# Four narrow products of a fused attention and FFN kernel on Trainium2: from 256 moving columns to the columns that are used

## The chip, the cores and the metric

The kernel runs on one core of one Trainium2 chip. The time is device time in microseconds of one launch: 1570.47 us, the median of three runs (1569.87 to 1570.59).

## What is computed

The reference takes x (16 x 64 tokens of 512 features) and a context of the same size through eight residual layers; every layer first normalises x. Cut to what the change touches:

```python
x = x + L0_xattn(layernorm(x), ctx, ...)      # 32 heads, 4 kv heads
x = x + L0_ffn(layernorm(x), ...)             # base + 28 LoRA experts of rank 8, top 2
x = x + L1_xattn(layernorm(x), ctx, ...)
x = x + L1_ffn(layernorm(x), ...)             # base + 8 LoRA experts of rank 8, top 2
x = x + L2_xattn(layernorm(x), ctx, ctx)      # linear attention over the context
x = x + L2_ffn(layernorm(x), ...)             # 4 LoRA experts of rank 16, top 2
x = x + L3_xattn(layernorm(x), ctx, ...)      # one head of 512, keys of the own batch
x = x + L3_ffn(layernorm(x), ...)             # dense where similarity to 64 centroids is high

# L2 attention, the context product
kvs = einsum('bnhd,bnhe->bhde', softmax(k, over n), v)
# L2 FFN, the gate: 4 router logits and the 4*16 hidden values of the experts
logits = flat @ router_w.T;  mid = einsum('tf,erf->ter', flat, A)
# L3 attention, the scores
scores = einsum('btf,bsf->bts', Q, K) * scale
# L3 FFN, the similarity
dots = softmax(x @ centroids.T / TEMPERATURE)
```

## The kernel before

The 1024 tokens are eight tiles (NT = 8) of 128, two batches of 64 in each. x stays on the chip in `x_res` from the first layer to the last. A product of two fp32 numbers is made in three passes: each operand is split into a high and a low part, and `PASSES` names high x high, high x low and low x high. The contraction over 512 features is four slices (KT = 4), so a product of one tile is a group of 4 x 3 = 12 matmuls, each with its own weight load of 128 columns. ScalarE writes the high part of an operand, VectorE or GpSimd the low part (the helper line L1721 on VectorE, L1275 on ScalarE, L488 on GpSimd), and a semaphore counts tiles that are ready.

Each engine has its own instruction list, written out in the order in which it runs. On TensorE the order around the change is this.

- Both large attention layers (L0, L1) end at about 1300 us; the change does not touch them. The second FFN follows, with a gate of 72 columns (`gate_product`, L720), a dense product of 512 columns (L733) and an expert product (L971).
- `middle_step(t)` then interleaves three stages. For tile t it transposes exp(context) (L1044) and multiplies it with the context (L1080, `psK2`); for tile t-2 it multiplies the queries with the result (L1071 to L1073, 12 matmuls of 144 and 128 columns) and transposes the outcome (L1095). For tile e = t-5 it runs the gate of the third FFN (L720, out to `psSO`), and for e-1 the transposed hidden values (L955) and the expert product (L971, three matmuls of 512). For tile n = t-9 it runs the key product of the last attention (L1008, 512 columns). Transposes of normalised x are L706.
- `cross_attention` runs the last two layers over tiles p: `scores` (L1113), `q_transpose` (L1124), `q_proj` (L1137, 512 columns), a bias matmul (L1102), `k_transpose` (L1016), `p_transpose` (L1145), `similarity` (L1164), `attend` (L1152) and `dense` (L1181, 512 columns).

Four products in these stages move 256 columns for each matmul, though fewer are read:

- The context product L1080 needs its own tile's 128 columns; `two_tiles(t)` gives it two tiles of 128, and VectorE reads half of `psK2` (L2124).
- The gate of the third FFN needs 4 + 64 = 68 columns; `f.moving` is 2 * P for it, and the width for the other two.
- The scores L1113 need the 128 keys of their own tile; `kT3_pair` gives those of two tiles, and `own_scores` picks the half. For that the product waits until the keys of the next tile are there too.
- The similarity L1164 needs 64 centroids; the slice is 4 * S wide.

Of the kernel before, what the change touches and what calls it, by code (L numbers as in the profile page):

```python
# [5 lines left out]
P = 128  # L6
B, S, D = 16, 64, 512
TOK = B * S
NT = TOK // P
# [74 lines left out]
def build(nc, io):  # L84
# [94 lines left out]
    class Ffn:  # L179


        def __init__(self, index, ln, E, R, dense, scale, wkv_n, wo_n):
            self.index, self.ln, self.E, self.R = index, ln, E, R
            self.done = index * NT
            self.dense, self.scale = dense, scale
            self.width = E + E * R
            self.moving = self.width if dense else 2 * P
            self.parts = 2 if E * R > P else 1
            self.rows = E * R // self.parts
            self.wkv_n, self.wo_n = wkv_n, wo_n  # L190
# [40 lines left out]
    def lat(hl, k, n):  # L231
        return hT[:, hl, k, n, 1:3].rearrange("p b t -> p (b t)")
# [12 lines left out]
    def kT3(hl, n):  # L245
        return hT[:, hl, :, n, 0:4:3, :]

    def kT3_pair(hl, n, k):
        first = min(n, NT - 2)
        return hT[:, hl, k, first:first + 2, 0:4:3, :]  # L250

    def own_scores(n, b):
        at = (n == NT - 1) * P + b * S
        return psO[b * S:(b + 1) * S, 0, at:at + S]

    def two_by_two(t):
        return t[:].rearrange("p (b j c) -> p b j c", b=2, j=2)
# [47 lines left out]
    def gate_bank(f, n):  # L305
        return psS if f.index == 2 else psQ
# [7 lines left out]
    kvs_r = v1[:].rearrange("p a h c -> p (a h c)")[:, 0:4 * (P + GRP)].rearrange("p (a h c) -> p a h c", a=2, h=2)  # L314
    out_T = psTP[:].rearrange("p a (c t) -> p (a c) t", c=2)
    r_sum, y_T = k_sb[:, 0:S], prob[:]
    psE, psK2, psKT = psSO[:, 1], psSO[:, 2, 0:2 * P], psSO[:, 2]
    hidT = oT

    k3, k_in = prob, stage_q[:, 3]  # L320
# [373 lines left out]
    def _(pe):  # L694
# [14 lines left out]
        def gate_product(f, t):  # L709

            s, done = FS, f.done
            pe.wait_ge(LNS[f.ln]["lo"], ln_at(f.ln, t + 1))
            need(pe, s["hid"], done + t)
            if f.index == 2 and t == 0:
                pe.wait_ge(s["x_add"], done)
            if t == 0:
                pe.wait_ge(ld["wkv_lo"], f.wkv_n)
            for k in range(KT):
                for i, (xl, wl) in enumerate(PASSES):
                    m = mm(gate_bank(f, t)[:, 0:f.moving], lat(xl, k, t),  # L720
                           wkv[:, wl, k // 2, k % 2 * f.width:k % 2 * f.width + f.moving],
                           start=k == 0 and i == 0, stop=k == KT - 1 and i == 2)
            m.then_inc(s["gate_a"], 1)

# [272 lines left out]
            if 0 <= u < NT:  # L997
                experts(f, u)

        def two_tiles(n):  # L1000
            first = min(n, NT - 2)
            return slice(first * P, (first + 2) * P)

        def k_product(n):
            need(pe, N3["k_in"], n)
            for k in range(KT):
# [26 lines left out]
        def middle_step(t):  # L1033

            s, f, e, n = M, FF[2], t - 5, t - 9
            if 0 <= e - 1 < NT:
                if e == 5:
                    pe.wait_ge(s["y"], NT)
                hidden_transpose(f, e - 1)
            if t < NT:  # L1040
                pe.wait_ge(s["e"], t + 1)
                need(pe, s["eT_lo"], t)
                for k in range(KT):
                    i = tr(psE[:, k * P:(k + 1) * P], stage_q[:, t % 4, k * P:(k + 1) * P], ident[:])  # L1044
                i.then_inc(s["e_tr"], 1)
            if 0 <= t - 4 < NT:
                def free():
                    if t == 4:
                        pe.wait_ge(FS["hid"], 2 * NT)
                    need(pe, LNS[5]["lo"], ln_at(5, t - 4))  # L1050
                ln_transpose(5, t - 4, free)
            if 0 <= e < NT:
                if e <= 4:
                    need(pe, FS["hidT_lo"], f.done + e)
                gate_product(f, e)
            if 0 <= e - 1 < NT:
                experts(f, e - 1)
            if 0 <= n - 1 < NT:
                if n == 1:
                    pe.wait_ge(LNS[6]["lo"], ln_at(6, 2))  # L1060
                k_transpose(n - 1)
            if 0 <= t - 2 < NT:
                u = t - 2
                pe.wait_ge(s["q_lo"], u + 1)
                pe.wait_ge(s["kvs_lo"], u + 1)
                need(pe, s["y"], u)
                if u == 0:
                    pe.wait_ge(FS["hidT_lo"], 2 * NT)
                for c in range(KT):
                    q_of = lambda hl: q_e[:, hl, c * P:(c + 1) * P]  # L1070
                    mm(out_T[:, c, 0:P + GRP], q_of(HI), kvs_r[:, u % 2, HI, :], start=True, stop=False)  # L1071
                    mm(out_T[:, c, 0:P], q_of(HI), kvs_r[:, u % 2, LO, 0:P], start=False, stop=False)
                    m = mm(out_T[:, c, 0:P + GRP], q_of(LO), kvs_r[:, u % 2, HI, :], start=False, stop=True)  # L1073
                m.then_inc(s["out"], 1)
            if t < NT:
                pe.wait_ge(s["eT_lo"], t + 1)
                need(pe, s["kvs"], t)
                for k in range(KT):
                    for i, (el, cl) in enumerate(PASSES):
                        m = mm(psK2, eT[:, el, k, :], ctxT[:, cl, k, two_tiles(t)],  # L1080
                               start=k == 0 and i == 0, stop=k == KT - 1 and i == 2)
                m.then_inc(s["kv"], 1)
            if 0 <= n < NT:
                if n == 0:
                    pe.wait_ge(LNS[6]["lo"], ln_at(6, 1))
                    pe.wait_ge(ld["wo_lo"], 71)
                k_product(n)
            if 0 <= t - 2 < NT:
                u = t - 2
                pe.wait_ge(s["y"], u + 1)  # L1090
                need(pe, s["x_add"], u)
                if u == 0:
                    pe.wait_ge(FS["x_add"], 2 * NT)
                for c in range(KT):
                    i = tr(psY[:, c * P:(c + 1) * P], y_T[:, c * P:(c + 1) * P], ident[:])  # L1095
                i.then_inc(s["y_tr"], 1)
            if 0 <= e - 3 < NT:
                norm6_transpose(e - 3)
# [5 lines left out]
        def cross_attention(next_ln):  # L1104
            s = N3

            def scores(n):
                pe.wait_ge(s["qT_lo"], n + 1)
                pe.wait_ge(s["kT_lo"], min(n + 2, NT))
                need(pe, s["exp"], n)  # L1110
                for k in range(KT):
                    for i, (ql, kl) in enumerate(PASSES):
                        m = mm(psO[:, 0, 0:2 * P].rearrange("p (n b c) -> p n b c", n=2, b=2), qT3[:, ql, k, :],  # L1113
                               kT3_pair(kl, n, k), start=k == 0 and i == 0, stop=k == KT - 1 and i == 2)
                m.then_inc(s["scores"], 1)

            def q_transpose(n):
# [37 lines left out]
            def similarity(n):  # L1155

                pe.wait_ge(LNS[next_ln]["lo"], ln_at(next_ln, n + 1))
                if n == 0:
                    pe.wait_ge(ld["wkv_lo"], 33)
                    pe.wait_ge(FS["hid"], 3 * NT)  # L1160
                need(pe, C3["exp"], n)
                for k in range(KT):
                    for i, (xl, wl) in enumerate(PASSES):
                        m = mm(psS[:, 0:4 * S], lat(xl, k, n), wkv[:, wl, k // 2, k % 2 * S:k % 2 * S + 4 * S],  # L1164
                               start=k == 0 and i == 0, stop=k == KT - 1 and i == 2)
                m.then_inc(C3["sim"], 1)

# [106 lines left out]
    def _(act):  # L1274
# [344 lines left out]
        def cross_attention(next_ln):  # L1619
# [12 lines left out]
            def exps(n):  # L1632
                act.wait_ge(s["neg_max"], n + 1)
                need(act, s["p_tr"], n)
                for b in range(2):
                    rows = slice(b * S, (b + 1) * S)
                    i = nc.scalar.activation(s_sb[rows, b * S:(b + 1) * S], own_scores(n, b), ACT.Exp,
                                             bias=small[rows, 10:11], scale=small[rows, 9:10],
                                             accum_out=small[rows, 11:12])
                i.then_inc(s["exp"], 1)  # L1640
# [76 lines left out]
    def _(dve):  # L1717
# [387 lines left out]
        def middle_step(t):  # L2105
# [13 lines left out]
            if 0 <= t - 1 < NT:  # L2119
                dve.wait_ge(s["kv"], t)  # L2120
                link(V.reciprocal(small[:, 12:13], small[:, 10 + (t - 1) % 2:11 + (t - 1) % 2]))
                need(dve, s["kvs_lo"], t - 1)
                own = 0 if t < NT else P
                V.scalar_tensor_tensor(kvs, psK2[:, own:own + P], small[:, 12:13], block8[:], ALU.mult,  # L2124
                                       ALU.mult).then_inc(s["kvs"], 1)
            if 0 <= n - 1 < NT:
                k_norm(n - 1)
# [39 lines left out]
        def cross_attention(next_ln):  # L2167
# [6 lines left out]
            def row_max(n):  # L2174
                dve.wait_ge(s["scores"], n + 1)
                for b in range(2):
                    rows = slice(b * S, (b + 1) * S)
                    i = V.tensor_reduce(mx[rows, 0:1], own_scores(n, b), AX.X, ALU.max)
                link(i)
                V.tensor_scalar(col(10), mx[:, 0:1], col(9), -1.0, ALU.mult, ALU.mult).then_inc(s["neg_max"], 1)  # L2180

# [200 lines left out]
```

## Time and profile before

| | |
|---|---|
| median of 3 runs | 1570.47 us |
| the profiled execution | 1570.53 us |
| its span, first to last instruction | 1568.7 us |
| granted clock, mean over the span | 0.985 |
| TensorE matmul busy | 1501.3 us, 96% |
| VectorE busy | 1008.9 us, 64% |
| ScalarE busy | 821.1 us, 52% |
| GpSimd busy | 379.4 us, 24% |

Times in the rows are microseconds from the span's start. PE is TensorE's matmuls and PEld its weight loads, DVE is VectorE, ACT ScalarE, POOL GpSimd. Line numbers are those of the kernel before. A matmul's row counts a group of like matmuls, and its duration runs from the first start to the last end, so groups that follow each other overlap by the tail of the last matmul. PEclk is the granted share of TensorE's clock: 1.00 is 2.4 GHz, 0.50 is 1.2 GHz.

### The profile page before, as it was taken

How to read it: one execution, taken by the hardware profiler on the slowest of the kernel's cores; microseconds unless marked ns; L12 is line 12 of the kernel's file. 1: busy time of each engine (PE TensorE's matmuls, PEld its weight loads, DVE VectorE, ACT ScalarE, POOL GpSimd, SP SyncE). 2: the span in 40 equal slices, each digit the busy share in tenths (PEclk: the TensorE clock that was granted, in tenths of full speed). 3: DMA queues.
4: the chain of work that ended last, by engine and by line, in shares of the span. 5: the costliest groups of instructions: out<-in, count | busy, mean ns of one | idle time of the engine just before them, and what ended most of it. 6: DMA issues, size and time to landing. Idle time of an engine off the chain costs nothing.

```text
span 1568.7 us, 27791 instructions
## 1 busy us (share of the span) xinstructions
PE 1501.3 (96%) x9658; PEld 1323.4 (84%) x9658; DVE 1008.9 (64%) x2475; ACT 821.1 (52%) x2862; POOL 379.4 (24%) x388
## 2 busy tenths in 40 slices
PE   7999999999999998999999999999999998879896
PEld 7899999999999997788888888888888887667785
DVE  6666556655665568766665666656666677688775
ACT  4556445644555455346565556555565652554542
POOL 4102010201111011133232332323232321543420
PEclk9999999999999999999999999999999998799998
DMA  4100100100011001010101010101100001111001
GB/s 182 62 28 28 42 28 28 56 14 28 28 55 36 33 13 41 28 41 28 41 28 41 28 50 19 68 8 62 41 28 32 5 8 55 44 55 35 24 11 57
DMA packets 14624, 60.21 MB, mean 38 GB/s; under 512 B 2085, under 2 KB 3493, under 8 KB 9497
## 3 DMA queue, kind: packets, MB, share of 16 engines
q1 hardware_dynamic: 14488, 58.46, 10.5%
q8 instruction: 79, 1.29, 0.4%
q14 instruction: 57, 0.46, 0.1%
HBM read 56.36 MB, written 2.10 MB: 37 GB/s over the span
## 4 chain that ended last, share of the span: by engine, by line
PE 59%; issue 27%; DVE 7%; POOL 3%; ACT 2%; DMA 1%; POOLq 0%; DVEq 0%; SPq 0%; ACTq 0%
PE psY L869 15%; PE psQ L790 11%; PE psKV L812 8%; PE psSO L759 3%; PE psSO L856 2%; PE psTP L822 2%; PE psQ L775 2%; PE psTP L775 2%; PE psSO L760 2%; POOL wo L488 1%; PE psTP L840 1%; PE psKV L733 1%; PE psQ L1137 1%; PE psQ L720 1%; PE psTP L706 1%
## 5 line engine op out<-in xcount | busy, mean ns | idle before, releaser
L869 PE MATMUL psY<-wo,oT 128*128 128x512 f32 x1536 | 384.9, 399 | 1.8 <-DVE oT L1721 1.2
L869 PEld LDWEIGHTS psY<-wo,oT 128*128 128x128 f32 x1536 | 278.6, 188 | 65.8 <-POOL wo L488 2.2
L488 POOL TENSOR_TENSOR wo<-stage_o,wo 128x512 fp32r<-128x512 f32 (+2 forms) x71 | 91.1, 1309 | 309.0 <-ACT wo L1275 309.0
L1275 ACT ACTIVATE pT<-psTP 128x512 fp32r<-128x512 f32 (+1 forms) x128 | 62.8, 491 | 169.4 <-PE psTP L840 169.4
L593 POOL TENSOR_TENSOR rms<-ms_eps,minus_half 128x5 f32<-128x5 f32 x64 | 74.7, 1168 | 280.2 <-DVE ms_eps L1884 277.2
L1356 ACT ACTIVATE prob<-wide,neg_mx 128x128 f32<-128x128 f32 x256 | 99.8, 391 | 75.0 <-DVE neg_mx L1871 74.8
L1353 ACT ACTIVATE prob<-s_sb,neg_mx 128x64 f32<-128x64 f32 x256 | 86.0, 337 | 98.3 <-DVE neg_mx L1871 98.3
L1721 DVE TENSOR_TENSOR pT<-psTP,pT 128x512 fp32r<-128x512 f32 (+1 forms) x128 | 71.3, 557 | 77.4 <-ACT pT L1275 76.4
L1721 DVE TENSOR_TENSOR v<-psKV,v 128x128 fp32r<-128x128 f32 x64 | 18.7, 292 | 140.4 <-ACT v L1275 140.4
L812 PEld LDWEIGHTS psKV<-wkv,arena 128*128 128x128 f32 x768 | 99.8, 190 | 9.0 <-DVE kT L1908 4.6
L812 PE MATMUL psKV<-wkv,arena 128*128 128x256 f32 x768 | 103.4, 284 | 1.2 <-DVE kT L1908 1.2
L790 PE MATMUL psQ<-wq,hT 128*128 128x512 f32 x384 | 104.0, 408 | 0.0
L775 PE MATMUL psQ<-hT,wq 128*128 128x256 f32 x768 | 99.6, 285 | 4.2 <-DVE hT L1721 2.9
L790 PE MATMUL psQ<-hT 128*128 128x512 f32 x372 | 100.1, 407 | 0.0
L775 PEld LDWEIGHTS psQ<-hT,wq 128*128 128x128 f32 x768 | 94.9, 192 | 5.9 <-DVE hT L1721 3.1
L812 PE MATMUL psKV<-wkv,hT 128*128 128x256 f32 x768 | 99.8, 286 | 0.0
L775 PE MATMUL psTP<-hT,wq 128*128 128x256 f32 x768 | 99.1, 286 | 0.0
L1275 ACT ACTIVATE oT<-psSO 128x512 fp32r<-128x512 f32 (+1 forms) x132 | 76.4, 579 | 38.8 <-PE psY L869 32.1
L775 PEld LDWEIGHTS psTP<-hT,wq 128*128 128x128 f32 x768 | 96.0, 195 | 0.0
L812 PEld LDWEIGHTS psKV<-wkv,hT 128*128 128x128 f32 x768 | 94.1, 192 | 0.3
L1326 ACT ACTIVATE pT<-psQ 128x128 fp32r<-128x128 f32 x252 | 66.3, 280 | 53.4 <-PE psQ L790 53.4
L1721 DVE TENSOR_TENSOR oT<-psSO,oT 128x512 fp32r<-128x512 f32 (+1 forms) x132 | 88.7, 672 | 7.5 <-ACT oT L1275 7.2
(303 smaller groups left out, 3389.5 us busy)
## 6 DMA issues: line engine op xcount, KB each, us to landing
stage_o<-in_wo SPq DMA_DIRECT2D x16, 1024.0 KB, 4.8
stage_q<-in_wq SPq DMA_DIRECT2D x15, 1024.0 KB, 5.3
stage_kv<-in_wkv SPq DMA_DIRECT2D x12, 512.0 KB, 3.6
stage_q<-in_ctx SPq DMA_DIRECT2D x16, 256.0 KB, 2.8
stage_o<-in_ctxT SPq DMA_DIRECT2D x2, 1024.0 KB, 5.8
stage_q<-in_base SPq DMA_DIRECT2D x2, 1024.0 KB, 4.9
out<-x_res SPq DMA_DIRECT2D x8, 256.0 KB, 2.4
x_res<-in_x SPq DMA_DIRECT2D x1, 1536.0 KB, 11.1
```

The lines of the kernel that those rows point to most:

```text
L488: g.tensor_tensor(dst[LO], stage, dst[HI].bitcast(f32), ALU.subtract).then_inc(ld[done or what + "_lo"], 1)
L593: g.tensor_tensor(rms[:, t.res(2)], ms_eps[:, t.res(2)], minus_half[:, 0:5], ALU.pow).then_inc(s["rms"], 1)
L759: mm(bank[:, at:at + 2 * keys], q_of(HI), k_of(slice(0, 2)), start=True, stop=False)
L775: m = mm(out, wq[:, wl, c, head], lat_pair(xl, c, k.res(NT) // 2), start=c == 0 and i == 0, stop=c == KT - 1 and i == 2)
L790: m = mm(by_eight(q_bank(st)[:]), lat(xl, k, n), wq_slice(st.div(NT) + a.wq0, wl, k), start=k == 0 and i == 0, stop=k == KT - 1 and i == 2)
L812: m = mm(psKV[:, b * 256:(b + 1) * 256], lhsT, wkv_k(wl, k, 256), start=k == 0 and i == 0, stop=k == KT - 1 and i == 2)
L869: m = mm(psY[:], oT[:, ol, h, :], wo[:, wl, h, :], start=h == 0 and i == 0, stop=h == HQ - 1 and i == 2)
L1275: copy = lambda o, i: nc.scalar.activation(o, i, ACT.Copy)
L1326: i = nc.scalar.activation(junk_q[h], q_bank(st)[:, h * HD:(h + 1) * HD], ACT.Square, accum_out=ssq[:, n, h:h + 1])
L1353: e = nc.scalar.activation(prob[:, at], s_sb[:, at], ACT.Exp, bias=neg_mx[:, j:j + 1], scale=1.0, accum_out=sums[:, j:j + 1])
L1356: e = nc.scalar.activation(prob[:, at], wide[:, at], ACT.Exp, bias=neg_mx[:, j:j + 1], scale=a.scale, accum_out=sums[:, j:j + 1])
L1721: return V.tensor_tensor(dst_lo, src, dst_hi.bitcast(f32), ALU.subtract)
```

## The change

The four products move only the columns that are used: 128 for the context product, 68 for the gate of the third FFN, 128 for the scores, 64 for the similarity. The scores wait for the keys of their own tile alone. No instruction is added, taken away or moved on any engine; the operands of 32 groups of 12 matmuls get narrower, and VectorE and ScalarE read the same values from the place where they now lie.

```diff
@@ class Ffn
-            self.moving = self.width if dense else 2 * P
@@ helpers
-    def kT3_pair(hl, n, k):
-        first = min(n, NT - 2)
-        return hT[:, hl, k, first:first + 2, 0:4:3, :]
-
-    def own_scores(n, b):
-        at = (n == NT - 1) * P + b * S
-        return psO[b * S:(b + 1) * S, 0, at:at + S]
+    def own_scores(b):
+        return psO[b * S:(b + 1) * S, 0, b * S:(b + 1) * S]
@@
-    psE, psK2, psKT = psSO[:, 1], psSO[:, 2, 0:2 * P], psSO[:, 2]
+    psE, psK2, psKT = psSO[:, 1], psSO[:, 2, 0:P], psSO[:, 2]
@@ TensorE, gate_product
-                    m = mm(gate_bank(f, t)[:, 0:f.moving], lat(xl, k, t),
-                           wkv[:, wl, k // 2, k % 2 * f.width:k % 2 * f.width + f.moving],
+                    m = mm(gate_bank(f, t)[:, 0:f.width], lat(xl, k, t),
+                           wkv[:, wl, k // 2, k % 2 * f.width:k % 2 * f.width + f.width],
@@ TensorE, middle_step, the context product
-                        m = mm(psK2, eT[:, el, k, :], ctxT[:, cl, k, two_tiles(t)],
+                        m = mm(psK2, eT[:, el, k, :], ctxT[:, cl, k, tok(t)],
@@ TensorE, cross_attention, scores
-                pe.wait_ge(s["kT_lo"], min(n + 2, NT))
+                pe.wait_ge(s["kT_lo"], n + 1)
...
-                        m = mm(psO[:, 0, 0:2 * P].rearrange("p (n b c) -> p n b c", n=2, b=2), qT3[:, ql, k, :],
-                               kT3_pair(kl, n, k), start=k == 0 and i == 0, stop=k == KT - 1 and i == 2)
+                        m = mm(psO[:, 0, 0:P].rearrange("p (b c) -> p b c", b=2), qT3[:, ql, k, :],
+                               kT3(kl, n)[:, k], start=k == 0 and i == 0, stop=k == KT - 1 and i == 2)
@@ TensorE, cross_attention, similarity
-                        m = mm(psS[:, 0:4 * S], lat(xl, k, n), wkv[:, wl, k // 2, k % 2 * S:k % 2 * S + 4 * S],
+                        m = mm(psS[:, 0:S], lat(xl, k, n), wkv_k(wl, k, S),
@@ VectorE, middle_step
-                own = 0 if t < NT else P
-                V.scalar_tensor_tensor(kvs, psK2[:, own:own + P], small[:, 12:13], block8[:], ALU.mult,
+                V.scalar_tensor_tensor(kvs, psK2, small[:, 12:13], block8[:], ALU.mult,
```

The exponential on ScalarE and the row maximum on VectorE call `own_scores(b)` where they called `own_scores(n, b)`.

## Rows read from the trace of the kernel before

**Rows 1.** The page: busy time of TensorE, and the chain by engine.
```profile
PE 1501.3 (96%) x9658; PEld 1323.4 (84%) x9658; DVE 1008.9 (64%) x2475; ACT 821.1 (52%) x2862; POOL 379.4 (24%) x388
...
PE 59%; issue 27%; DVE 7%; POOL 3%; ACT 2%; DMA 1%; POOLq 0%; DVEq 0%; SPq 0%; ACTq 0%
```

**Rows 2.** Busy time by stretches: length, PE, PEld, DVE, ACT, POOL, PEclk, DMA, GB/s.
```profile
1348.60:1365.70 17.10, 13.24 (x61) 12.43 (x61) 7.40 (x19) 7.53 (x17) 9.23 (x12) 0.50 0.11 33
1365.70:1410.00 44.30, 35.02 (x262) 30.36 (x261) 38.87 (x122) 28.03 (x62) 18.82 (x29) 1.00 0.20 65
...
1441.00:1536.30 95.30, 89.11 (x485) 71.55 (x484) 67.63 (x167) 49.32 (x126) 32.41 (x45) 1.00 0.09 27
1536.30:1539.80 3.50, 3.50 (x15) 3.21 (x15) 1.72 (x4) 0.00 (x0) 0.77 (x2) 0.51 0.02 5
```

**Rows 3.** TensorE's timeline (start, duration, what), score products of 256 columns and their successors.
```profile
1456.92 1.60 PE L1113 MATMUL psSO<-hT,qT 128*128 128x256 f32 x12
1458.35 0.60 PE L1124 MATMUL psTP<-ident,q_sb 128*128 128x128 f32 x4
...
1493.96 1.70 PE L1113 MATMUL psSO<-hT,qT 128*128 128x256 f32 x12
1495.50 0.60 PE L1124 MATMUL psTP<-ident,q_sb 128*128 128x128 f32 x4
```

**Rows 4.** TensorE's timeline at the full clock: a 72-column gate, an output product.
```profile
1327.60 1.51 PE L720 MATMUL psQ<-wkv,hT 128*128 128x72 f32 x12
1328.94 2.98 PE L733 MATMUL psY<-hT 128*128 128x512 f32 x12
...
1378.15 0.23 PE L1071 MATMUL psTP<-v,qT 128*128 128x144 f32 x1
...
1379.44 1.64 PE L1080 MATMUL psSO<-arena,kT 128*128 128x256 f32 x12
```

**Rows 5.** The chain that ended last, in order of time (start, duration, what).
```profile
1361.52 2.65 PE psSO L1080 x12
...
1554.25 1.63 PE psSO L1164 x12
```

**Rows 6.** TensorE's timeline in the stretches at half clock and at their ends.
```profile
1313.50 2.75 PE L720 MATMUL psQ<-wkv,hT 128*128 128x72 f32 x12
1316.06 5.42 PE L733 MATMUL psSO<-hT 128*128 128x512 f32 x12
...
1358.68 0.49 PE L1071 MATMUL psTP<-v,qT 128*128 128x144 f32 x1 [1.68 <-POOL qT L659]
...
1361.32 2.86 PE L1080 MATMUL psSO<-arena,kT 128*128 128x256 f32 x12
1363.97 1.06 PE L1095 MATMUL psY<-ident,prob 128*128 128x128 f32 x4
...
1410.26 2.93 PE L720 MATMUL psSO<-wkv,hT 128*128 128x256 f32 x12 [3.66 <-DVE oT L1721]
1413.12 1.11 PE L971 MATMUL psKV<-wkv,oT 64*128 64x512 f32 x3
1414.15 0.33 PE L1071 MATMUL psTP<-v,qT 128*128 128x144 f32 x1
...
1415.55 2.98 PE L1008 MATMUL psSO<-wo,arena 128*128 128x512 f32 x12
...
1537.48 2.60 PE L1164 MATMUL psSO<-wkv,hT 128*128 128x256 f32 x12
```

**Rows 7.** Busy time just before the clock fell at 1311.1 us, columns as in rows 2.
```profile
1307.50:1311.00 3.50, 3.12 (x19) 2.15 (x17) 3.18 (x12) 0.85 (x4) 0.00 (x0) 1.00 0.94 356
```

**Rows 8.** TensorE's timeline: gates of two successive steps of the middle stage.
```profile
1383.89 1.68 PE L720 MATMUL psSO<-wkv,hT 128*128 128x256 f32 x12 [0.34 <-DVE oT L1721]
...
1391.59 1.67 PE L720 MATMUL psSO<-wkv,hT 128*128 128x256 f32 x12
```

**Rows 9.** TensorE's timeline: the wait behind 1540 us.
```profile
1546.88 0.98 PE L1152 MATMUL psY<-oT,pT 128*128 128x512 f32 x3 [1.50 <-DVE pT L1721]
```

More of the change, by code:

```diff
@@ L998, in ffn_step @@
                 experts(f, u)
-        def two_tiles(n):
-            first = min(n, NT - 2)
-            return slice(first * P, (first + 2) * P)
         def k_product(n):
@@ L1636, in exps @@
                     rows = slice(b * S, (b + 1) * S)
-                    i = nc.scalar.activation(s_sb[rows, b * S:(b + 1) * S], own_scores(n, b), ACT.Exp,
+                    i = nc.scalar.activation(s_sb[rows, b * S:(b + 1) * S], own_scores(b), ACT.Exp,
                                              bias=small[rows, 10:11], scale=small[rows, 9:10],
@@ L2177, in row_max @@
                     rows = slice(b * S, (b + 1) * S)
-                    i = V.tensor_reduce(mx[rows, 0:1], own_scores(n, b), AX.X, ALU.max)
+                    i = V.tensor_reduce(mx[rows, 0:1], own_scores(b), AX.X, ALU.max)
                 link(i)
```

## The prediction

> **What bounds the kernel now.** I read the busy shares and the chain of waits on the page first. TensorE is busy 1501.3 of 1568.7 us, and its own work makes up 59% of the chain that ended last [rows 1]. The whole change lies on that engine, in 32 groups of twelve matmuls: eight token tiles by four products. So the questions are how long such a group takes, and in which of the late stages TensorE sets the pace.
>
> The table by stretches, cut where the granted clock changes, answers the second [rows 2]. The four products stand between 1347 and 1556 us. From 1365.7 to 1410 us, in the middle stage, VectorE is busy 38.87 of 44.3 us and TensorE 35.02: at the full clock VectorE leads there. Behind 1441 us TensorE is busy 89.11 of 95.3 us and leads. The column to look at is PEclk. It is 1.00, the 2.4 GHz level, in most stretches, and 0.50, the 1.2 GHz level, from 1348.6 to 1365.7 us and in a short one at 1536 (another, behind 1410 us, shows in rows 6 by a gate of 2.93 us for 1.68).
>
> The timeline of TensorE gives the time of a group, taken from one group's start to the start of the next that follows without idle time (a row's own duration also holds the last matmul's tail).
>
> **First part: what the columns cost at the full clock.** The diff takes columns away and no instruction: weight loads, their number and their order stay. With 256 columns a group takes 1458.35 - 1456.92 = 1.43 us or 1495.50 - 1493.96 = 1.54 us [rows 3]. No narrowed product is in the trace as such, but its neighbours are. The gate of the second FFN, with 72 columns, takes 1328.94 - 1327.60 = 1.34 us, and the twelve matmuls of the middle stage's output product, with 144 and 128 columns, take 1379.44 - 1378.15 = 1.29 us [rows 4]. That is 0.11 us for each matmul whether it moves 72 or 144 columns: a floor, and the weight load that stands before every one of these matmuls is what stays. So a group saves between 0.09 us (1.43 - 1.34) and 0.25 us (1.54 - 1.29); I take the middle, 0.17. All 32 groups: 5.4 us. On the path lie fewer. The chain passes through two context products, two gates, seven score products and three similarity products, 14 in all, of which the rows show the first and the last [rows 5]: 14 x 0.17 = 2.4 us saved. The bounds are 0 and 5.4 us, since the others run where VectorE or a wait ends later.
>
> The Trainium skill (TensorE: Matmul & The Clock Gate, section "Back-to-back issue gap") gives a sustained 81 ns for a matmul of 128 columns with its weight load. Twelve would take 0.97 us, and the 32 groups would save some 16 us. The rows do not agree: they show 110 ns.
>
> The score product now waits for one tile of keys where it waited for two. Its rows carry no idle time before them [rows 3], so that is worth nothing. VectorE and ScalarE read the same 128 or 64 columns as before, and nothing moves on any queue.
>
> **Second part: the granted clock.** What did TensorE do before the clock rose? The first of the late rises came after a group of 512 columns (L733, 5.42 us for 2.98). At 1365.7 us it rose after a context product of 256 columns (L1080) and transposes. About 1413 us it rose after a gate of 256 columns (L720, 2.93 us), and at 1539.8 us after a similarity product of 256 columns (L1164, 2.60 us) [rows 2, 4, 6]. Three of these four groups are among those that the change narrows. The narrow output product (L1071 to L1073) ran at half clock from 1358.68 to 1361.32 us without a pause and the clock stayed down; it came back after the wide group that followed. In the stretch before the fall at 1311 us TensorE was busy 3.12 of 3.50 us, with a 72-column gate among this work [rows 7]: a busy engine alone did not keep the clock. From 1365.7 to 1410 us the clock held with TensorE busy 79% of the time, and there the wide context products and gates stand between narrow ones and transposes. After the change almost everything in this stage is narrow; only three matmuls of L971 in a step move 512 columns. So I expect the clock to fall there again and again, and to rise late.
>
> Two rates bound the price. At the full clock a step of this stage takes 1391.59 - 1383.89 = 7.70 us [rows 8]. At half clock the pieces have rows [rows 6]: a narrow gate 1316.06 - 1313.50 = 2.56 us, three matmuls of L971 at 5.42 / 12 = 0.45 each 1.36, the output product 1361.32 - 1358.68 = 2.64, the context product 1363.97 - 1361.32 = 2.65 with 256 columns and by the gate's row 2.56 with 128. Thirteen transposes (L1095, L1044, L706, L955) take 0.213 each, the pace of the gate's matmuls, so 2.77. The sum is 11.89 us: TensorE would then lead the stage, and the step costs 4.19 us more. From 1365.7 to 1406.6 us, where TensorE's work ends ahead of a wait of 3.66 us, 5.3 such steps pass. With the clock never falling they cost 0, with it always at half 22 us. I take half of the time, since each step still holds L971 and thirteen transposes that may bring the clock back: **11 us**.
>
> Then the two rises that hang on wide groups. At 1410 us the narrow gate leaves the clock down for what follows: L971 takes 0.33 us more (1.36 - 1.03), the output product 1.24 us more (2.64 - 1.40), and half of the key product L1008, 512 columns, 1.2 (half of 5.42 - 2.98). Together **2.8 us**. At 1536 us the score product runs at half (2.56 for 1.43) and half of L1181 (512 columns, 1.2 as above) as well, 2.3 us, of which the wait of 1.50 us further on takes in a part [rows 3, 6, 9]: **1.5 us**. Between 1420 and 1480 us the gates and similarity products become narrow beside idle time, and I count **1.4 us** for one or two falls there. Bounds for these three together: 0 and 11 us.
>
> Sum: 1570.5 - 2.4 + 11 + 2.8 + 1.5 + 1.4 = 1584.8, say 1585 us. It is made against the profiled execution, 1570.53 us (span 1568.7 and 1.83 us around it); the median of the runs shown is 1570.47, the same.
>
> **Rivals.** A, the clock does not care. The narrow groups keep TensorE issuing almost as long as before, so the clock keeps its old pattern, and only the first part remains: 1570.5 - 2.4 = 1568.1 us, down to 1565.1 if all 32 groups count. For it: the clock held for 95 us behind 1441, with many groups of 128 columns among the work. Against it: rows 6 and 7. It decides if the profile after has PEclk 1.00 through the middle stage. The Trainium skill (the same page, section "The HAM clock gate") has the clock gated by how busy the engine has been, and would, read as time spent on instructions, give this case; row 7's fall, with the engine busy 89% of the stretch, speaks against that reading.
>
> B, the clock suffers only at the two late rises. The middle stage holds its clock as before, and the terms of 2.8 and 1.5 us stand beside the 2.4 saved: 1572.4 us, with 1570.5 to 1576. For it: L971 and the transposes remain in every step. Against: the clock fell at 1311 us with L971 in the work of that stretch.
>
> C, time goes by the columns. If a group's time fell with its columns, the context and score groups would save 0.7 us each and the narrower ones 1.07, 28 us in all; 14 us of it on the path would give 1556 us. The skill's smaller figure above points this way. The 72-column rows exclude it nearly.
>
> **How the numbers follow.** My forecast, more time at the half clock in the middle stage, has 0.70 of the chance and reaches from 1574 (a quarter of the time at half, the late terms small) to 1602 (1570.5 + 22 + 11 - 2.4 = 1601). A has 0.15, B 0.14, C 0.01. The range 1570 to 1602 leaves out most of A, all of C and a little above, less than 0.2. A change of 0.2%, 3.1 us, is about what a measurement of this kernel can tell from none. C and the part of A that saves over 3.1 us give 0.05 for faster. The rest of A and nearly half of B give 0.17 for the same. The remainder is 0.78 for slower.
>
> **What would show it.** PEclk between 1365 and 1410 us well below 1, and the span from the first context product to the last gate longer by some 10 us, with L1044, L1071 and L706 slower though untouched. In the rows where the clock is full, narrowed groups should take 1.29 to 1.34 us from start to start. The rise that stood at 1413.5 us should come during L1008. Everything before 1347 us should stay as it was. I am wrong if the stage keeps its clock (A), or if the clock is down and the time is the same, which would mean that TensorE's longer groups fit under VectorE's 38.87 us.

## The result and the profile after

The changed kernel takes 1579.27 us (median of seven runs, 1578.09 to 1586.87); the kernel before, in as many runs, 1570.59 (1569.87 to 1574.84). The ratio is 1.0061, with a 95% interval of 1.0048 to 1.0074: slower by 9.6 us by the ratio, between 7.5 and 11.6 (the two medians differ by 8.7). The profiled execution has a span of 1578.3 us against 1568.7.

First the lines of the profile's page that answer to [rows 1], with the granted clock in 40 slices, in tenths of full speed. Line numbers are now those of the changed kernel, 6 to 10 lower in this part: L714 is the gate, L1070 the context product, L1103 the scores, L1154 the similarity.

```profile
PE 1514.0 (96%) x9658; PEld 1335.0 (85%) x9658; DVE 1008.0 (64%) x2475; ACT 821.8 (52%) x2862; POOL 379.8 (24%) x388
...
PEclk9999999999999999999999999999999998688998
...
PE 61%; issue 26%; DVE 7%; POOL 3%; ACT 2%; DMA 1%; POOLq 0%; DVEq 0%; SPq 0%; ACTq 0%
```

TensorE has as many instructions as before, narrower ones among them, and is busy 12.7 us longer (1514.0 for 1501.3). VectorE and ScalarE are within 1 us. That alone points at TensorE's rate. The table by stretches, cut where the clock changes, shows it (length, then PE, PEld, DVE, ACT and POOL busy, PEclk, DMA share, GB/s; compare [rows 2]):

```profile
1350.70:1374.60 23.90, 19.82 (x93) 19.02 (x93) 12.02 (x29) 11.67 (x26) 11.81 (x16) 0.50 0.21 62
1374.60:1405.30 30.70, 26.81 (x207) 23.53 (x206) 28.44 (x93) 20.65 (x47) 12.31 (x21) 1.00 0.11 35
1405.30:1412.10 6.80, 5.38 (x25) 4.74 (x24) 4.95 (x16) 2.12 (x4) 1.78 (x1) 0.50 0.08 10
1412.10:1415.50 3.40, 0.90 (x8) 0.90 (x9) 2.01 (x6) 1.46 (x3) 2.25 (x4) 1.00 0.73 289
1415.50:1425.80 10.30, 10.30 (x33) 8.32 (x33) 4.90 (x19) 0.91 (x2) 1.63 (x4) 0.50 0.00 1
...
1446.30:1449.70 3.40, 3.40 (x10) 2.63 (x9) 1.79 (x8) 0.49 (x2) 3.04 (x4) 0.50 0.00 0
...
1487.20:1490.60 3.40, 3.40 (x10) 2.67 (x9) 2.26 (x7) 0.21 (x2) 0.61 (x2) 0.50 0.06 21
...
1555.50:1562.30 6.80, 6.80 (x26) 5.92 (x25) 3.87 (x11) 1.41 (x4) 0.98 (x2) 0.50 0.00 0
```

From 1350 us to the end of TensorE's work the clock is at half for 54.6 us (23.9 + 6.8 + 10.3 + 3.4 + 3.4 + 6.8). Before it was 24.1 (17.1 and 3.5 in [rows 2], and 3.5 near 1410, in this row of the trace before):

```profile
1410.00:1413.50 3.50, 3.25 (x13) 3.02 (x14) 1.38 (x6) 0.37 (x1) 0.91 (x3) 0.51 0.13 54
```

Below, a change of the clock from full to half is called a fall and one from half to full a rise.

TensorE's timeline at the places of [rows 3, 4, 6]:

```profile
1363.44 2.75 PE L1070 MATMUL psSO<-arena,kT 128*128 128x128 f32 x12
1365.98 1.07 PE L1085 MATMUL psY<-ident,prob 128*128 128x128 f32 x4
...
1402.67 1.53 PE L714 MATMUL psSO<-wkv,hT 128*128 128x68 f32 x12
...
1414.60 1.95 PE L714 MATMUL psSO<-wkv,hT 128*128 128x68 f32 x12 [2.55 <-DVE oT L1711]
...
1420.69 5.32 PE L998 MATMUL psSO<-wo,arena 128*128 128x512 f32 x12
...
1465.99 1.45 PE L1103 MATMUL psSO<-hT,qT 128*128 128x128 f32 x12
1467.28 0.62 PE L1114 MATMUL psTP<-ident,q_sb 128*128 128x128 f32 x4
...
1521.75 1.50 PE L1154 MATMUL psSO<-wkv,hT 128*128 128x64 f32 x12
1523.09 0.95 PE L1142 MATMUL psY<-kT,pT 128*128 128x512 f32 x3
```

At the full clock the narrowed groups are shorter, as costed: scores 1467.28 - 1465.99 = 1.29 us, similarity 1523.09 - 1521.75 = 1.34. What stands beside them is not: the key product L998, untouched, takes 5.32 us where it took 2.98 [rows 6].

Where the 9.6 us between the two profiled executions (spans 1578.3 and 1568.7) came in follows from the starts of the same groups in both traces. The first context product starts 2.1 us later (1349.96 for 1347.84), before any changed instruction has run. In this execution the clock also fell near 620 and 709 us, in work that is the same in both kernels.

```profile
619.00:625.00 6.00, 6.00 (x38) 5.87 (x37) 5.21 (x11) 2.24 (x5) 0.55 (x1) 0.72 0.41 164
...
708.00:713.00 5.00, 3.91 (x14) 3.33 (x15) 2.71 (x8) 4.53 (x15) 2.20 (x3) 0.66 0.00 0
```

No changed instruction had run by then, and in the profiles of the other kernels these two falls are there or not, so I put them down to the execution; with one profile of each kernel that is argued, not shown. Of the other 7.5 us, 1.4 come in up to the gate at 1402.67 (1399.11 before), 3.9 more up to the gate behind the first key product (1427.19 for 1419.71), 1.6 up to the first query projection (1450.74 for 1441.65). From there to the last score product 1.1 us are won (1547.89 for 1539.92), and 1.6 lost behind it.

### The profile page after: what moved, and what is told of

Read it like the earlier page. It is cut to its first block, busy times and chain, and to the rows that moved or that the text cites. A ratio compares the mean times of both kernels' runs of the same rounds, so it can differ in the third digit from the quotient of the medians.

```text
span 1578.3 us, 27791 instructions
## 1 busy us (share of the span) xinstructions
PE 1514.0 (96%) x9658; PEld 1335.0 (85%) x9658; DVE 1008.0 (64%) x2475; ACT 821.8 (52%) x2862; POOL 379.8 (24%) x388
## 3 DMA queue, kind: packets, MB, share of 16 engines
q8 instruction: 79, 1.29, 0.3%
## 4 chain that ended last, share of the span: by engine, by line
PE 61%; issue 26%; DVE 7%; POOL 3%; ACT 2%; DMA 1%; POOLq 0%; DVEq 0%; SPq 0%; ACTq 0%
PE psY L863 15%; PE psQ L784 11%; PE psKV L806 8%; PE psSO L753 3%; PE psSO L850 2%; PE psTP L816 2%; PE psQ L769 2%; PE psSO L754 2%; PE psTP L769 2%; POOL wo L482 1%; PE psTP L834 1%; PE psKV L1171 1%; PE psQ L714 1%; PE psKV L727 1%; PE psQ L1127 1%
```

## Experiments: one product at a time

Two theories are tested. The clock theory: narrow groups cost nothing themselves, but TensorE's clock falls more often and rises later with them. Its rival: the narrow groups or the changed order of waits cost time in some other way. Four kernels narrow one product each. All ratios are to the kernel before, run on the same chip beside them. The diffs are cut to the lines that matter.

**Context product alone.**

```diff
-                        m = mm(psK2, eT[:, el, k, :], ctxT[:, cl, k, two_tiles(t)],
+                        m = mm(psK2, eT[:, el, k, :], ctxT[:, cl, k, tok(t)],
```

> Only the context product (L1080) is narrowed to 128 columns; gate, scores and similarity stay at 256. Clock theory: the late rise in the middle stage (1365.7 us before, 1374.6 us in the changed kernel) hangs on this product, so it comes back here: the half-clock stretch that begins near 1349 us is 20 us or longer against 17.1 before, and the kernel is 1 to 4 us slower than before. Rival, the time comes from the gate or from the late stages: the stretch stays at 17 us and the time is within 1 us of before.

Measured: 1577.87 us, ratio 1.0033 (1.0018 to 1.0048), so 5 us slower. The stretch table of its profile:

```profile
1347.30:1381.40 34.10, 30.44 (x143) 29.64 (x143) 19.53 (x46) 18.30 (x42) 15.85 (x23) 0.50 0.16 49
1381.40:1408.70 27.30, 23.36 (x174) 20.01 (x173) 24.67 (x88) 15.91 (x36) 8.72 (x15) 1.00 0.11 39
1408.70:1425.80 17.10, 14.27 (x51) 11.80 (x50) 8.83 (x28) 2.96 (x6) 5.65 (x8) 0.50 0.17 62
```

The stretch at half is twice as long as before, as the clock theory wants. It is longer even than the changed kernel's 23.9 us: where exactly the clock rises differs from profile to profile. The last row shows more than was expected. Near 1410 us the clock was down for 17.1 us, although the gate there is wide as before, and the key product ran at half:

```profile
1413.94 2.93 PE L720 MATMUL psSO<-wkv,hT 128*128 128x256 f32 x12 [2.83 <-DVE oT L1721]
...
1421.01 5.18 PE L1008 MATMUL psSO<-wo,arena 128*128 128x512 f32 x12
```

A wide group is therefore not enough to bring the clock back.

**Gate alone.**

```diff
-            self.moving = self.width if dense else 2 * P
+            self.moving = self.width
```

> Only the gate of the third FFN (L720, out to psSO) is narrowed to 68 columns. Clock theory: the stretch up to 1410 us is as before, with the rise near 1366 us, but the gate behind the wait of 3.7 us near 1410 us no longer brings the clock back, which stays at half through the output product and the key product L1008: 3 to 5 us slower than before. Rival, a narrower gate is only shorter work: 0 to 1 us faster.

Measured: 1577.0 us, ratio 1.0035 (1.0022 to 1.0048), 5.5 us slower and a little above the expected range. The place near 1410 us on TensorE's timeline, and its stretch:

```profile
1409.21 2.77 PE L720 MATMUL psSO<-wkv,hT 128*128 128x68 f32 x12 [2.54 <-DVE oT L1721]
1411.92 1.64 PE L971 MATMUL psKV<-wkv,oT 64*128 64x512 f32 x3
1416.12 4.51 PE L1008 MATMUL psSO<-wo,arena 128*128 128x512 f32 x12
```

```profile
1402.40:1419.40 17.00, 13.22 (x48) 11.29 (x49) 10.37 (x30) 4.13 (x8) 5.65 (x8) 0.50 0.19 62
```

With the wide gate the clock was back when the output product began [rows 6]; with the narrow one it returns only in the key product, and it had fallen 7.6 us earlier too (1402.4 for 1410.0 us). In the run before this one the same happened behind a wide gate, so the width of the gate alone does not explain this place; each of the two products, narrowed alone, went with a stretch of 17 us here in its profile.

**Scores alone.**

```diff
-                pe.wait_ge(s["kT_lo"], min(n + 2, NT))
+                pe.wait_ge(s["kT_lo"], n + 1)
-                               kT3_pair(kl, n, k), start=k == 0 and i == 0, stop=k == KT - 1 and i == 2)
+                               kT3(kl, n)[:, k], start=k == 0 and i == 0, stop=k == KT - 1 and i == 2)
```

> Only the scores (L1113) are narrowed to 128 columns and wait for one tile of keys. Clock theory: TensorE's other work in this stage is 512 columns wide, so the clock keeps its pattern of before, and seven groups on the path save 0.14 us each: 1 us faster, 0 to 2. Rival, any narrow product costs clock: one or more falls between 1441 and 1536 us and 1 to 3 us slower.

Measured: 1570.91 us against 1572.5 before in the same job, ratio 0.9993 (0.9985 to 1.0002): 1.1 us faster, with an interval that just holds no change. It is the only one of the four that does not cost. The first fall behind 1441 us, 6.8 us long, is at 1465, beside a wait of 2.65 us, as the rival expected; but the one at 1536 us is gone, and a fall of 6.8 us at this wait stands also in the profile of a kernel with wide scores (the wide one with dummies below, at 1462 us).

**Similarity alone.**

```diff
-                        m = mm(psS[:, 0:4 * S], lat(xl, k, n), wkv[:, wl, k // 2, k % 2 * S:k % 2 * S + 4 * S],
+                        m = mm(psS[:, 0:S], lat(xl, k, n), wkv_k(wl, k, S),
```

> Only the similarity product (L1164) is narrowed to 64 columns. Clock theory: one more fall near 1475 to 1485 us, where the first similarity stands beside a wait, and a later rise behind the fall near 1536 us, together 2 to 4 us, less 0.5 us for the shorter groups: 1 to 3 us slower. Rival, no fall there by this product alone: 0.5 to 1 us faster.

Measured: 1574.76 us, ratio 1.0018 (1.0009 to 1.0027), 2.8 us slower. The first fall behind 1441 us came where it was expected, behind the first similarity and the wait, and the one near 1540 us lasted 6.9 us for 3.5:

```profile
1477.26 1.50 PE L1164 MATMUL psSO<-wkv,hT 128*128 128x64 f32 x12
1479.57 1.38 PE L1152 MATMUL psY<-oT,pT 128*128 128x512 f32 x3 [0.81 <-DVE pT L1721]
```

```profile
1479.90:1483.30 3.40, 3.40 (x9) 2.62 (x8) 2.14 (x7) 0.38 (x2) 0.41 (x1) 0.50 0.10 37
1493.60:1497.00 3.40, 3.40 (x10) 2.62 (x9) 2.26 (x7) 0.21 (x2) 0.58 (x2) 0.50 0.09 32
1541.30:1548.20 6.90, 6.90 (x30) 6.50 (x29) 4.14 (x13) 1.35 (x4) 1.08 (x3) 0.51 0.01 2
```

The four effects, 5.2 + 5.5 - 1.1 + 2.8, make 12.4 us; together the edits cost 9.6 (7.5 to 11.6). The stretch near 1410 us fits that: 17.1 and 17.0 us at half in the two profiles with the context product or the gate alone narrow, 6.8 + 10.3 with both, as if it were paid once. Each of the four effects has an interval of 1.3 to 2.4 us to either side, so the difference of 2.8 us is not itself shown.

## Experiments: giving TensorE other work

**Narrow context product, its columns given back as dummies.** The added (dummy) matmuls write a part of the output tile `psSO` that nobody reads.

```diff
                 need(pe, s["kvs"], t)
+                for _ in range(4):
+                    mm(psSO[:, 2, P:4 * P], ctxT[:, HI, 0, 0:P], ctxT[:, HI, 0, 0:3 * P], start=True, stop=True)
                 for k in range(KT):
```

> The context product is narrowed to 128 columns as in the run with it alone, and in front of each of its eight groups stand four dummy matmuls of 384 columns (1536 columns, as many as the narrowing took away), written to a part of the bank that nobody reads. They cost TensorE 0.7 us each group at the full clock and more at half, so the engine has more to do than before or with the narrow product alone. Clock theory: the clock comes back as before, the half-clock stretch that begins near 1349 us is at most 21 us where it was 34 us with the narrow product alone, and the time falls by 1 to 4 us below that run's 1577.9 in spite of the added work. Rival, narrow groups cost time in another way than by the clock: the dummies only add, 1578 to 1583 us.

Measured: 1576.63 us, ratio 1.0029 (1.0018 to 1.0041). The stretch at half is 20.5 us in its profile, as expected:

```profile
1350.10:1370.60 20.50, 18.26 (x81) 17.46 (x80) 8.72 (x22) 8.24 (x20) 9.68 (x13) 0.50 0.10 29
```

The time is 1.2 us below that of the narrow product alone, although at least 5.6 us of work were added (eight groups at 0.7 us); but the two kernels were timed on different chips, and by the ratios, whose intervals overlap, it is 0.6 us. The clock moved as foreseen, in one profile; the time does not decide.

**Dummies in the waits of the middle stage**, with wide products, with all four narrow, and with only the scores narrow. Nobody reads them.

```diff
+        def filler(bank, count):
+            for _ in range(count):
+                mm(bank, ctxT[:, HI, 0, 0:P], ctxT[:, HI, 0, 0:D], start=True, stop=True)
...
                 i.then_inc(s["e_tr"], 1)
+                if t < 3:
+                    filler(psQ[:], (6, 9, 7)[t])
...
             if 0 <= e < NT:
+                if t == 9:
+                    filler(psT, 14)
```

> The kernel before, all products at 256 columns, with dummy matmuls of 512 columns in TensorE's idle time of the middle stage: 6, 9 and 7 behind the context transposes of the first three steps, 14 in front of the gate that waits near 1410 us; nobody reads them. Clock theory: the stretch at half clock from 1349 to 1366 us and the one at 1410 us vanish or shrink to one of 7 us at most, 3 to 7 us faster than before. Rival, TensorE's clock in these idle stretches is worth nothing, since others lead there: the same, or 1 us slower.

Measured: 1569.33 us against 1571.02, ratio 0.9977 (0.9965 to 0.9988): 3.6 us faster by the ratio. The stretch table, where before PEclk stood at 0.50 for 17.1 us:

```profile
1345.00:1366.00 21.00, 17.14 (x109) 14.07 (x110) 13.77 (x34) 12.84 (x31) 13.01 (x18) 1.00 0.19 59
1366.00:1408.00 42.00, 36.40 (x263) 31.21 (x262) 36.72 (x115) 26.31 (x59) 17.66 (x26) 1.00 0.18 60
1408.00:1440.00 32.00, 29.49 (x173) 24.30 (x174) 27.55 (x93) 14.88 (x35) 11.99 (x20) 1.00 0.06 16
1440.00:1561.00 121.00, 111.95 (x581) 89.31 (x580) 79.59 (x204) 52.44 (x137) 32.85 (x47) 0.94 0.06 21
```

More work on the busiest engine made the kernel faster. What it bought is the clock: averaged over the executions it is 0.989 here and 0.984 before.

> The changed kernel, all four products narrow, with the same dummy matmuls. Clock theory: the fill takes away the stretch at 1349 us and the one at 1410 us, and with them most of what the change cost; the falls behind 1440 us stay. 1567 to 1572 us, so 7 to 12 us below the changed kernel's 1579.3. Rival, the change costs by something else than the clock: it stays 8 to 9 us above the filled kernel with wide products.

Measured: 1580.25 us, ratio 1.0046 (1.0031 to 1.0062). A miss: it stayed where the changed kernel is. Its profile has the stretch of 17 us gone, but PEclk is below 1 in every stretch from 1300 us on. The first of them is no different from before, the other three are:

```profile
1300.00:1342.00 42.00, 37.86 (x192) 29.85 (x191) 30.54 (x124) 8.98 (x28) 10.22 (x15) 0.88 0.15 51
1342.00:1406.00 64.00, 55.52 (x360) 47.33 (x360) 50.86 (x158) 39.69 (x92) 29.60 (x43) 0.91 0.14 44
1406.00:1438.00 32.00, 30.13 (x162) 25.28 (x160) 23.33 (x76) 12.86 (x29) 11.70 (x18) 0.86 0.12 42
1438.00:1560.00 122.00, 112.75 (x572) 90.97 (x572) 80.85 (x213) 55.26 (x145) 37.11 (x52) 0.91 0.07 21
```

The kernel before has in the first of these stretches

```profile
1300.00:1342.00 42.00, 37.85 (x191) 29.79 (x190) 31.83 (x131) 9.84 (x32) 10.69 (x16) 0.88 0.15 51
```

With the same dummies the narrow kernel is 10.8 us slower than the wide one by the two ratios, about as much as without them. By its time alone this run would speak for the rival. The next section shows why it does not.

> The filled kernel with wide products and only the scores narrow. Clock theory: the two gains add, 1 us below the filled wide kernel, and 4 to 8 us below the kernel before. Rival: with the fill gone by, the scores' narrowing costs clock behind 1441 us, and it is slower than the filled wide kernel by 1 us or more.

Measured: 1566.74 us, ratio 0.9969 (0.9958 to 0.998), 4.9 us faster than before, in the expected range. Against the wide kernel with the same dummies it gains 1.3 us by the two ratios, as expected, though the intervals overlap.

## Time against clock, over all executions

Every timed execution has its own mean granted clock. Twelve executions of the narrow kernel with dummies, and others for comparison:

```
kernel                                    us at mean granted clock
all four narrow, dummies in the middle    1570.91 at 0.985; 1573.60 at 0.982; the other ten 1579.75 to 1582.55 at 0.974 to 0.978
before (wide)                             1570.81 at 0.985; 1573.55 at 0.982; 1569.22 at 0.987
changed                                   1578.09 at 0.977; 1580.11 at 0.973; 1586.87 at 0.967
context product alone narrow              1573.84 at 0.982; 1580.53 at 0.973
wide, dummies in the middle               1565.97 at 0.992; 1571.16 at 0.988
```

At the same clock the kernel with four narrow products and the wide one take the same time within what executions at one clock differ by. The two of the narrow one, 1570.91 us at 0.985 and 1573.60 at 0.982, lie inside those of the kernel before, 1570.16 to 1573.57 at 0.985 and 1572.14 to 1576.14 at 0.982. A straight line through all 204 timed executions whose clock is on record, of the kernel before and the thirteen others, has a slope of 0.87 us for each 0.001 of clock and a correlation of -0.97, and no kernel's mean lies more than 1.2 us off it. 0.001 of the mean clock is 3.1 us at half rate, so a microsecond at half costs about 0.28 us. Applied to the two profiles: 54.6 - 24.1 = 30.5 us more at half, times 0.28, is 8.5 us, less 1 to 2 us for the shorter groups; 7.5 us were found. The two halves of this agree, but the slope was fitted to these executions too, so this is no second proof.

The mean clock also goes with what was narrowed, over 6 to 12 executions of each changed kernel and 80 of the one before: 0.984 before, 0.985 with the scores narrow, 0.982 with the similarity, 0.978 with the gate, 0.977 with the context product, 0.973 with all four. Together with the dummies, which add work and give time back, this shows that the clock carries the loss. Whether the shorter groups save the 2.4 us that were costed it does not tell: the executions at one clock spread by more. What sets the moments at which it falls in one execution and not in the next stays open.

## Experiments: looking for a better version

The last four kernels carry the dummies of the middle stage and more. First, ten in the fourth step of the second FFN:

```diff
+            if f.index == 1 and t == 3:
+                for _ in range(10):
+                    mm(psSO[:, 1], ctxT[:, HI, 0, 0:P], ctxT[:, HI, 0, 0:D], start=True, stop=True)
```

> The filled kernel with narrow scores, and ten more dummy matmuls of 512 columns in the wait of 2.1 to 2.6 us of the second FFN's fourth step (near 1311 us), where every profile so far has a stretch of 10 us at half clock. Clock theory: that stretch goes, L720 takes 1.5 us there for 2.75 and L733 3.0 for 5.4, and the kernel is 2 to 4 us below the 1566.7 of the run without these ten. Rival, the stretch is led by another engine: the same time.

Measured with narrow scores: 1567.02 us (1563.46 to 1569.82), ratio 0.9969 (0.9959 to 0.9979), the same as without these ten. In its profile the stretch is down from 10 us to 3.4, and L732, the dense product, takes 3.03 us; but the dummies themselves ran at half, 4.09 us for ten. The profiled execution is the fastest of the ten, at a mean clock of 0.993; the others go down to 0.987, with 1569.82 us for the slowest. So the profile shows the stretch gone in one good execution, and the expected 2 to 4 us did not come in the median. What the slower ones lost, and where, was not found.

```profile
1309.82 4.09 PE L981 MATMUL psSO<-arena 128*128 128x512 f32 x10
...
1313.78 1.55 PE L719 MATMUL psQ<-wkv,hT 128*128 128x72 f32 x12
1315.17 3.03 PE L732 MATMUL psSO<-hT 128*128 128x512 f32 x12
```

Then dummies also in three waits of `attend`:

```diff
             def attend(n):
+                need(pe, s["x_add"], n)
+                for _ in range({1: 10, 6: 7, 7: 5}.get(n, 0)):
+                    mm(psY[:], wq[:, HI, 0, 0:P], wq[:, HI, 0, :], start=True, stop=True)
                 pe.wait_ge(s["pT_lo"], n + 1)
                 pe.wait_ge(s["f_lo"], n + 1)
-                need(pe, s["x_add"], n)
```

> As the run before, and dummy matmuls also in three waits of the last attention's attend (10, 7 and 5 of them, near 1460, 1530 and 1541 us). Clock theory: the falls at 1532 and 1542 us go, each worth 1 to 1.5 us: 1560 to 1563 us, the best of all. Rival, the dummies there hold up the attend behind them and nothing is gained: 1563 to 1566 us.

Measured with narrow scores: 1566.63 us (1562.46 to 1568.69), ratio 0.9962 (0.9948 to 0.9976). The expectation, 1560 to 1563 us, was missed, and the time is nearer to the rival's range. In its profile the two falls at 1532 and 1542 us are gone (PEclk 1.00 from 1470 to 1560 us), as foreseen, and one of 3.4 us near 1460 us stays beside the dummies there; the gain is 1.1 us by the ratios against the run before, with intervals that overlap. That the falls went and the time did not follow by as much is left open.

> All four products narrow, with all dummy matmuls. Clock theory: the falls beside the waits go, those in the middle of TensorE's work, where narrow groups and transposes follow each other without a wait worth filling, stay: 4 to 12 us above the kernel with the same dummies and only the scores narrow, with a mean granted clock below 0.985. Rival, the waits alone make the falls: within 1 us of it.

Measured: 1569.2 us (1566.69 to 1577.48), ratio 0.9988 (0.9976 to 1.0001). All four products are narrow, as in the changed kernel, and against the kernel before the loss is made up: 11.5 us less than the changed kernel by the two ratios (0.9988 and 1.0061). Part of that is what dummies give any of these kernels. Against the run before, with context product, gate and similarity wide and the same dummies, it is 2.6 us slower by the medians and 4.1 by the ratios, at the lower edge of the expected 4 to 12; the mean clock is 0.986 against 0.992, and below 0.985 was expected. Against the next run, which differs in context product and gate alone, it is 5.5 us slower by the ratios, with intervals that do not overlap: the narrowing still costs, a good half of the 9.6 us.

> Scores and similarity narrow, context product and gate wide, with all dummy matmuls. Clock theory: the similarity costs clock only beside the waits near 1475 and 1530 us; with the latter filled it costs 0 to 2 us against the kernel with only the scores narrow, where it cost 2.8 us without the fill. Rival, it saves what its shorter groups promise: 0.5 us faster.

Measured: 1564.47 us (1563.85 to 1566.39, five runs), ratio 0.9953 (0.9941 to 0.9966). The best of all: 7.4 us faster than before and, by the two ratios, 17 us (9.6 + 7.4) faster than the changed kernel. That the similarity costs nothing here was the rival's expectation, not mine (0 to 2 us slower). The mean clock is 0.993 against 0.992 without the narrow similarity, so it was kept up; that the narrow product is then only shorter is the likely reading. The interval overlaps with that of the run with the same dummies and only the scores narrow, so the 2.2 us between the medians (1.4 by the ratios) are not shown. The stretches from 1300 us on:

```profile
1300.00:1342.00 42.00, 39.72 (x212) 30.55 (x210) 33.85 (x142) 11.74 (x37) 13.47 (x19) 1.00 0.15 51
1342.00:1406.00 64.00, 55.77 (x376) 47.55 (x377) 50.92 (x149) 38.96 (x88) 30.62 (x44) 0.97 0.19 61
1406.00:1438.00 32.00, 29.45 (x171) 23.83 (x169) 27.56 (x92) 15.41 (x37) 12.10 (x20) 1.00 0.07 17
1438.00:1560.00 122.00, 110.14 (x599) 87.23 (x599) 82.30 (x208) 52.19 (x134) 32.82 (x46) 0.98 0.09 33
```

## Why the prediction was right, and where not

The direction was right, and that TensorE's clock carries the loss. Where it is lost was forecast wrong for the largest term. The time, 1579.3 for 1585, lies in the range, with some luck: the range is wide, the middle stage cost 1.4 us for the 11 forecast, the late stages more than forecast, and 2.1 us came from falls ahead of the change. Added up, the two profiles differ by 2.1 + 1.4 + 3.9 + 1.6 - 1.1 + 1.6 = 9.5 us, where the forecast has -2.4 + 11 + 2.8 + 1.5 + 1.4 = 14.3.

- The price at the full clock was right. The floor read from the 72-column gate and the output product held: 1.29 us with 128 columns, 1.34 with 64. Scores alone saved 1.1 us (seven groups at 0.14 make 1.0), with an interval that just holds nothing. That all fourteen groups on the path together save 2.4 us was not measured. The time by columns (rival C) and the 81 ns of the Trainium skill (TensorE: Matmul & The Clock Gate, section "Back-to-back issue gap") are excluded for this stream by 1.29 us for twelve, 108 ns each. Rival C's sum was wrong as well: by its own prices the fourteen groups on the path, nine at 0.7 and five at 1.07 us, save 11.7 us and not 14, which gives 1559 us.
- The argument from what stood before each rise holds in part. With the context product narrow the rise of 1365.7 us came later, with the gate narrow the clock stayed down behind 1410 us, and with the similarity narrow the stretch near 1540 us grew from 3.5 to 6.9 us. But with the context product alone narrow the clock also stayed down through the key product behind a wide gate, and in the changed kernel's profile there is no fall at all at the place of the one at 1536 us.
- The middle stage was mis-sized, the step "I take half of the time", worth 11 us. In the changed kernel's profile 1.4 us came in there, and the span from the first context product to the last gate is 5.4 us longer, not 10. From 1365 to 1410 us PEclk is 0.84, for 0.99 before. From 1374.6 to 1405.3 us the clock stood at full although context products and gates were narrow; it did not fall again and again, and why it held there is open. The price of a step was too high as well, because it was made from a full step. The first steps have neither gate nor L971, and other engines lead them. The third to fifth context products start at 1361.32 us [rows 6] and then at

```profile
1367.87 1.71 PE L1080 MATMUL psSO<-arena,kT 128*128 128x256 f32 x12 [0.73 <-DVE kT L1721]
...
1372.86 1.70 PE L1080 MATMUL psSO<-arena,kT 128*128 128x256 f32 x12
```

before, and in the run with this product alone narrow at

```profile
1360.48 2.75 PE L1080 MATMUL psSO<-arena,kT 128*128 128x128 f32 x12
...
1367.22 2.75 PE L1080 MATMUL psSO<-arena,kT 128*128 128x128 f32 x12
...
1374.81 2.75 PE L1080 MATMUL psSO<-arena,kT 128*128 128x128 f32 x12
```

  The first step was mostly at half in both (6.55 and 6.74 us; before, the clock rose at 1365.7); the second takes 7.59 us at half for 4.99 at full, 2.6 us more and not 4.2.
- The term at 1410 us was too small: 2.8 forecast, 3.9 found in the changed kernel (the narrow gate alone made the whole kernel 5.5 us slower), since the clock was down before the gate too and the key product ran at half for nearly all of its 5.32 us, not for half of it. The sign for this place held: the rise came at 1425.8 us, in the key product that began at 1420.69.
- The further falls (1.4 forecast) were there: one at 1446 us, with which 1.6 us came in, and one at 1487. For the last rise 1.5 us were forecast and 1.6 found behind the last score product, but that is chance: they came with another fall, from 1555.5 to 1562.3 us.
- Rival A, the clock does not care, is excluded by the stretch table, though its sign, a clock of 1.00 in the middle stage, held from 1374.6 to 1405.3 us. Rival B, only the two late rises suffer, comes nearest to where the changed kernel's profile lost its time; its price, 1572.4 us, was too low.
- "Everything before 1347 us should stay as it was" did not hold in the profile: 2.1 us of the 9.6 came in ahead of the change. The executions timed spread by more than some of the terms that I argued over.

## What to carry over

In this stream a matmul with a weight load before it had a floor of about 0.11 us at the full clock, the same for 64 to 144 columns; below it, fewer columns saved nothing on the engine, and they cost the clock for the untouched work that followed. Before narrowing a product, look at which groups stand just before each rise of PEclk, and at which waits follow it; that shows where to look, not how long the clock will stay down. Where TensorE waits for another engine at a place on which the clock hangs, dummy matmuls that nobody reads can pay for themselves, as 36 of them did here (3.6 us with wide products). Time them in several executions, since one profile shows one pattern of falls, and compare kernels at their mean granted clock.

## What was not expected of the hardware

The same kernel runs with different patterns of the clock: the changed one took 1578.09 us at a mean of 0.977 and 1586.87 at 0.967. The stretch at half that begins near 1350 us lasted 23.9 us in one kernel's execution and 34.1 in that of a kernel with fewer narrow products. In some profiles the clock fell near 620 and 709 us, in work that no kernel here changed, and in others not. For a change of a few microseconds this spread is as large as the effect.
